# Rewriting most stages of a decoder layer: biases in PSUM, quarter-array scores, norms on GpSimd, one GELU, a 16-bit down product

## Chip, cores and metric

The kernel runs on one core of one Trainium2 chip. The metric is the device time of the whole program in microseconds (us). The engines are PE (TensorE), DVE (VectorE), ACT (ScalarE), POOL (GpSimd) and SP (SyncE, which only issues DMA here).

## What is computed

One pre-norm decoder layer on x of shape (16, 64, 256):

```python
x = x + attn(layernorm(x))        # 16 heads of 16, causal, ALiBi, Wq/Wk/Wv/Wo with biases
x = x + xattn(layernorm(x), ctx)  # softmax(x @ ctx.T / 16, masked) @ ctx, one head of 256
x = x + ffn(layernorm(x))         # gelu(x @ up + b) @ down + b, F = 1024

def quantize_to_mxfp4(w, block_size=32):     # both FFN weights, at run time
    wb = w.reshape(K // 32, 32, N)
    scales = 2 ** (floor(log2(max(abs(wb), axis=1))) - 2)
    q = nearest value of (0, 0.5, 1, 1.5, 2, 3, 4, 6) with sign, of wb / scales
    return q, scales                          # the product uses q * scales
```

## The kernel before

The 1024 tokens lie in 8 tiles of 128 (two batches of 64 each), `x_sb`. The program is a list of named stages. `stages()` gives each its engine, an estimated time, what it must follow and which PSUM banks it writes; `schedule()` lays them out greedily with a time for each, with `URGENCY` as a table of priorities; every engine then walks the one list and issues its own stages in that order. Semaphores do the waiting.

- Layer norm (LN1, LN2, LN3), per tile: `stats` and `norm` on DVE (L776, L777, L785), `rstd` on POOL (L528, L532), `turn` transposes on PE (L932), `turn_copy` on ACT (L573, L576). For LN3, `low` on DVE (L791) keeps the rest that 16 bits lose, since the up product runs twice in fp16, high and low.
- Projections per half (4 tiles), with fp32 weights: `q` and `k` (L945) and `v` (L955). The keys are copied from `k_flat` into `k2`, 8 masked copies of 512 columns for each half and chunk `c`, on ACT (L598) and DVE (L799), shared out by `K_HEADS`: copy j keeps head j's 16 rows of the 128 and zeroes the others. So one product of `q_T` with `k2` gives eight heads' scores. The values go to `v2` half by DVE (L812), half by ACT, a DMA between partitions and ACT again (L609, L623).
- Attention in 16 units (tile, c): `scores` (L969), two products for the two batches, each 128 rows by 64 columns of the array with 512 columns streamed, into bank 0 or 1; `add_max` on DVE adds the ALiBi and causal table and takes the maximum (L825, L828); `centre` on POOL subtracts it (L556); `exp` on ACT (L629); `prob_T`, `prob_copy`, `pv`, `normalise`, `attn_turn`, `attn_copy` (L977, L636, L990, L838 and L839, L999, L643); per tile `out_proj` and `x1` (L1006, L846).
- Cross-attention per tile: `x_scores`, `x_mask` (adds the mask and takes the maximum on DVE, L865 and L869), `x_exp`, `x_prob_T`, `x_read`, `x_scale` (with the product with `valid`, L876), `x2`.
- Quantising: `amax`, `binade` and transposes give scales, `spread` (L1046, L1051) spreads them over rows. `quant` is four blocks on DVE, two per weight matrix, each of eight operations on two pieces of 512 columns and one on 1024 (L734 to L762). `raw` is one buffer, loaded four times.
- FFN in 32 blocks (4 groups of two tiles, 8 chunks): `up` (L1064, 4 products of 256 columns), `gelu` twice on ACT from the same bank (L688: one rounded to fp32r as `h_hi`, one full as `h_sb`), `split` on DVE (L902, the difference, `h_lo`), `down` (L1080, 4 fp32r products), then `final` (L909) and the store.

The stage of the scores, and the table which shares out the keys:

```python
for b in range(2):
    tok = slice(t * P + b * S, t * P + (b + 1) * S)
    last = pe.matmul(dst[b * S:(b + 1) * S, :].rearrange("p (h k) -> p h k", h=HC), q_T[:, c, tok],
                     k2[:, c, :, tok], start=True, stop=True)
...
K_HEADS = {(0, 0): 3, (0, 1): 3, (1, 0): 4, (1, 1): 4}
```

## Time and profile before

| | us |
|---|---|
| median of 3 runs (lowest, highest) | 159.94 (157.6, 162.42) |
| span of the profiled execution, first to last instruction | 157.1 |
| lowest run above that span | 0.5 |
| median run above that span | 2.8 |

The times of the three runs are of whole executions. The profile is of one execution, of which the page gives the span; what lies around it isn't given for it, so the differences above are to other executions. A duration in the profile is that of one instruction; on PE the ends are modelled and neighbours overlap, so the time that a matmul takes in a row of others is better read from one start to the next. An fp32 matmul shows as two records.

### The profile page before, as it was taken

How to read it: one execution, taken by the hardware profiler on the slowest of the kernel's cores; microseconds unless marked ns; L12 is line 12 of the kernel's file. 1: busy time of each engine (PE TensorE's matmuls, PEld its weight loads, DVE VectorE, ACT ScalarE, POOL GpSimd, SP SyncE). 2: the span in 40 equal slices, each digit the busy share in tenths (PEclk: the TensorE clock that was granted, in tenths of full speed). 3: DMA queues.
4: the chain of work that ended last, by engine and by line, in shares of the span. 5: the costliest groups of instructions: out<-in, count | busy, mean ns of one | idle time of the engine just before them, and what ended most of it. 6: DMA issues, size and time to landing. Idle time of an engine off the chain costs nothing. (4 is left out here: it accounts for less than half of the span.)

```text
span 157.1 us, 2931 instructions
## 1 busy us (share of the span) xinstructions
PE 127.9 (81%) x878; PEld 87.3 (56%) x878; DVE 126.1 (80%) x345; ACT 96.4 (61%) x212; POOL 54.1 (34%) x92
## 2 busy tenths in 40 slices
PE   0149999987992497991977999898999999979992
PEld 0027444312471174550565657677788989759991
DVE  1854998799999999779899988796785789697551
ACT  3014559996936045582322742666989899899970
POOL 8969920052211240310403343732540254052000
PEclk9999999999999789998579999999999999999999
DMA  4999993000020341910000000000000000020011
GB/s 95 321 329 341 368 274 144 2 2 4 2 67 0 87 180 30 280 30 0 0 0 4 0 0 0 4 2 0 4 0 2 4 33 31 3 73 0 0 67 67
DMA packets 9135, 11.20 MB, mean 71 GB/s; under 512 B 1665, under 2 KB 7937, under 8 KB 8993
## 3 DMA queue, kind: packets, MB, share of 16 engines
q1 hardware_dynamic: 7776, 9.90, 20.3%
q10 hardware_dynamic: 1344, 1.13, 2.2%
q8 instruction: 7, 0.11, 0.3%
q14 instruction: 8, 0.06, 0.1%
HBM read 9.45 MB, written 1.05 MB: 67 GB/s over the span
## 5 line engine op out<-in xcount | busy, mean ns | idle before, releaser
L556 POOL TENSOR_TENSOR s_sb<-s_sb,s_max 128x512 f32<-128x512 f32 x16 | 17.3, 1084 | 50.1 <-DVE s_max L828 50.1
L969 PE MATMUL bank<-k,q_T 128*64 128x512 f32 x64 | 20.0, 681 | 5.2 <-DVE s_sb L825 5.2
L1064 PE MATMUL bank<-xn_T,w_T 128*128 128x256 f16 x128 | 19.2, 273 | 1.2 <-ACT h_sb L688 0.7
L1080 PE MATMUL bank<-w_down_q,h_hi 128*128 128x256 f32 x64 | 18.7, 318 | 0.0
L636 ACT ACTIVATE p_T<-bank 128x512 f32<-128x512 f32 x16 | 9.6, 599 | 13.1 <-PE bank L990 10.3
L932 PE MATMUL bank<-const,xn 128*128 128x128 f32 x48 | 10.3, 304 | 8.8 <-DVE xn L785 8.7
L990 PEld LDWEIGHTS bank<-v,p_T 128*64 128x64 f32 x256 | 14.1, 148 | 5.9 <-issue 4.7
L902 DVE TENSOR_TENSOR h_lo<-h_sb,h_hi 128x256 fp32r<-128x256 f32 x32 | 13.4, 437 | 4.8 <-ACT h_sb L688 4.8
L528 POOL TENSOR_SCALAR var_eps<-mean_var 128x1 f32<-128x1 f32 x24 | 5.8, 240 | 31.7 <-DVE mean_var L777 31.6
L688 ACT ACTIVATE h_hi<-bank,bias_cols 128x256 fp32r<-128x256 f32 x32 | 15.3, 478 | 2.3 <-PE bank L1080 0.7
L990 PE MATMUL bank<-v,p_T 128*64 128x34 f32 x256 | 15.7, 235 | 1.2 <-ACT q_T L643 1.1
L1080 PE MATMUL bank<-w_down_q,h_lo 128*128 128x256 f32 x64 | 16.3, 282 | 0.0
L945 PE MATMUL bank<-xn_T,w_T 128*128 128x512 f32 x32 | 15.0, 600 | 0.3 <-ACT q_T L582 0.2
L688 ACT ACTIVATE h_sb<-bank,bias_cols 128x256 f32<-128x256 f32 x32 | 15.2, 475 | 0.0
L785 DVE TENSOR_SCALAR xn<-x_sb,mean_var,rstd 128x256 f32<-128x256 f32 x24 | 12.6, 524 | 3.1 <-PE bank L932 2.0
L532 POOL TENSOR_TENSOR rstd<-var_eps,minus_half 128x1 f32<-128x1 f32 x24 | 13.8, 575 | 2.0
L629 ACT ACTIVATE s_sb<-s_sb 128x512 f32<-128x512 f32 x16 | 10.0, 624 | 6.5 <-POOL s_sb L556 6.4
L776 DVE BATCH_NORM_STATS2 stats<-x_sb 128x6 f32<-128x256 f32 x24 | 10.0, 416 | 4.5 <-DMA x_sb<-in_x_dram 4.5
L932 PEld LDWEIGHTS bank<-const,xn 128*128 128x128 f32 x48 | 6.4, 153 | 12.5 <-issue 9.6
L1064 PEld LDWEIGHTS bank<-xn_T,w_T 128*128 128x128 bf16 x128 | 10.9, 97 | 4.4 <-issue 2.6
L1080 PEld LDWEIGHTS bank<-w_down_q,h_hi 128*128 128x128 f32 x64 | 12.1, 190 | 0.3
L1080 PEld LDWEIGHTS bank<-w_down_q,h_lo 128*128 128x128 f32 x64 | 12.2, 190 | 0.1
(82 smaller groups left out, 271.6 us busy)
## 6 DMA issues: line engine op xcount, KB each, us to landing
raw<-in_W_up_T_dram SPq DMA_DIRECT2D x1, 1024.0 KB, 10.5
ctx_T<-in_ctx_by_feature_dram SPq DMA_DIRECT2D x1, 1024.0 KB, 9.7
ctx_sb<-in_ctx_dram SPq DMA_DIRECT2D x1, 1024.0 KB, 9.9
raw<-in_W_up_dram SPq DMA_DIRECT2D x1, 1024.0 KB, 4.9
raw<-in_W_down_T_dram SPq DMA_DIRECT2D x1, 1024.0 KB, 4.8
raw<-in_W_down_dram SPq DMA_DIRECT2D x1, 1024.0 KB, 6.6
out_dram<-x_sb SPq DMA_DIRECT2D x8, 128.0 KB, 1.7
x_sb<-in_x_dram SPq DMA_DIRECT2D x4, 128.0 KB, 3.1
```

What stands on the lines that cost most here:

```text
L532: pool.tensor_tensor(rstd[:, n, t:t + 1], var_eps[:, n, t:t + 1], minus_half[:, :], ALU.pow).then_inc(rstd_ready[n], 1)
L556: pool.tensor_tensor(tile, tile, s_max[:, u % S_RING, :].unsqueeze(2).broadcast_to([P, HC, S]), ALU.subtract).then_inc(centred, 1)
L629: act.activation(s_sb[:, u % S_RING, :], s_sb[:, u % S_RING, :], ACT.Exp).then_inc(exp_ready, 1)
L688: act.activation(dst, bank[i % 2][:, 0:GN], ACT.Gelu_apprx_tanh, bias=bias_cols[:, BUP + f:BUP + f + 1], scale=1.0 / ACT_SCALE).then_inc(g ...
L785: dve.tensor_scalar(xn[:, ring[t % len(ring)], :], x_sb[:, t, :], mean_var[:, n, t, 0:1], rstd[:, n, t:t + 1], ALU.subtract, ALU.mult).the ...
L902: dve.tensor_tensor(h_lo[:, i % H_RING, :], h_sb[:, i % GELU_RING, :], h_hi[:, i % H_RING, :].bitcast(F32), ALU.subtract).then_inc(split_r ...
L932: last = pe.transpose(dst[:, c * P:(c + 1) * P], xn[:, ring[t % len(ring)], c * P:(c + 1) * P], ident)
L945: last = pe.matmul(dst[:, :], w_T[:, m, i, c * P:(c + 1) * P], half_tokens(h, i), start=(i == 0), stop=(i == EC - 1))
L969: last = pe.matmul(dst[b * S:(b + 1) * S, :].rearrange("p (h k) -> p h k", h=HC), q_T[:, c, tok], k2[:, c, :, tok], start=True, stop=True)
L990: last = pe.matmul(dst[b * S:(b + 1) * S, g * width:(g + 1) * width], p_T[:, u % 2, g, b * S:(b + 1) * S], v2[:, 2 * t + b, c * 4 + g, :, ...
L1064: last = pe.matmul(dst[:, 0:GN], w_up_q[:, c, f * P:(f + 1) * P], xn_T16[:, g * GT:(g + 1) * GT, at16:at16 + P], start=(k == 0), stop=(k = ...
L1080: last = pe.matmul(dst, src[:, i % H_RING, t * P:(t + 1) * P], w_down_q[:, f, :], start=(f == 0 and part == 0 and t == 0), stop=(f == FC - ...
```

## The change

Nearly all stages are rewritten, and the order is new:

- The ALiBi and causal table is split once into a high fp32r part and its rest (`bias_hi` on ACT, `bias_lo` on DVE) and added by PE: `s_bias`, a product of `twin` and `s_bias` into the bank, ahead of the scores. `scores` is now per tile for both units: 8 products of 64 rows, 64 columns of the array and 256 streamed columns, over the array's four quarters; `k2` has 4 masked copies (`SLOTS`) in place of 8. DVE takes the maximum from PSUM (`s_max`) and subtracts it (`s_sub`); `centre` is gone.
- The 16 key copies are shared among ACT (5), DVE (4) and POOL (7) by `K_ENGINE`; the key bias goes into `k_flat`.
- `v` writes even heads to partitions 0 to 63 and odd ones to 64 to 127, in products of 64 columns of the array; `v_even` (ACT) and `v_odd` (DVE) copy them in place, with no DMA. The value bias is folded into bo (`bo_fold`, `bo_sum`).
- The norms of LN2 and LN3 are on POOL, with a `shift` before them. `attn_turn` and `attn_copy` are per tile. The mask of the cross-attention is added by PE from a 16-bit product; `valid` is in the scale of `x_prob_copy`.
- Quantising is single stages (`quant`, 10 and 11 steps) of 2048 columns (the first two of 1024) in order with others; W_up has two buffers, `raw_T` and `raw`, and both its loads are issued at the start.
- FFN in 24 blocks: one group of 4 tiles (512 columns), two of 2. One GELU; `hi` (ACT in the first 8 blocks, POOL in the 16 behind them) scales it to fp16, `lo` (DVE) takes the rest, and `down` is 16-bit: fp16 times bf16.

```diff
+GROUPS = ((0, 1, 2, 3), (4, 5), (6, 7))
+K_ENGINE = {(0, 0): ("act", "act", "dve", "dve"), (0, 1): ("act", "pool", "dve", "dve"),
+            (1, 0): ("pool", "pool", "pool", "act"), (1, 1): ("pool", "pool", "pool", "act")}
+HI_ENGINE = ["act" if i < FC else "pool" for i in range(len(BLOCKS))]
...
 URGENCY = {
-    "x_fill": 23, "add_down": 23, "v2_zero": 22, "norm": 18, "q": 17, "turn": 16, "attn_copy": 14,
...
+    "add_bo": -20.1, "add_down": -25.3, "amax": 1.3, "attn_copy": -12.8, "attn_turn": -57.7, "bias_hi": 20.5,
...
+                if stage == "s_bias":
+                    t, r = at
+                    pe.wait_ge(twin_ready, 1)
+                    pe.wait_ge(s_bias_lo, 1)
+                    dst = claim(r, (subtracted, EC * t + r + 1))
+                    pe.matmul(dst[:, :], twin[:, :], s_bias[:, r * HU * S:(r + 1) * HU * S], start=True, stop=False,
+                              skip_group_check=True)
...
-                    dst = claim(u % 2, (scores_added, u + 1))
-                    for b in range(2):
-                        tok = slice(t * P + b * S, t * P + (b + 1) * S)
-                        last = pe.matmul(dst[b * S:(b + 1) * S, :].rearrange("p (h k) -> p h k", h=HC), q_T[:, c, tok],
-                                         k2[:, c, :, tok], start=True, stop=True)
+                    for c in range(EC):
+                        for r in range(EC):
+                            for b in range(2):
+                                tok = slice(t * P + b * S, t * P + (b + 1) * S)
+                                part = slice(r * S, (r + 1) * S)
+                                last = pe.matmul(
+                                    bank[r][b * S:(b + 1) * S, c * SLOTS * S:(c + 1) * SLOTS * S].rearrange(
+                                        "p (h k) -> p h k", h=SLOTS),
+                                    q_T[part, c, tok], k2[part, c, :, tok], start=False, stop=(c == EC - 1),
+                                    skip_group_check=True)
...
+                if stage == "norm" and at[0] != LN1:
...
+                    pool.tensor_scalar(xn[:, ring[t % len(ring)], :], x_sb[:, t, :], rstd[:, n, t:t + 1],
+                                       shift[:, n, t:t + 1], ALU.mult, ALU.add).then_inc(xn_ready[n], 1)
...
+                    for j in k_slots(h, c, "pool"):
+                        last = pool.tensor_scalar(k2[:, c, j, h * HT:(h + 1) * HT], k_flat[:, c, :],
+                                                  slot_mask[:, j:j + 1], 1.0, ALU.mult, ALU.mult)
...
-                    for dst in (h_hi[:, i % H_RING, :], h_sb[:, i % GELU_RING, :]):
-                        act.activation(dst, bank[i % 2][:, 0:GN], ACT.Gelu_apprx_tanh, bias=bias_cols[:, BUP + f:BUP + f + 1],
-                                       scale=1.0 / ACT_SCALE).then_inc(gelu_ready, 1)
+                    act.activation(h_sb[:, i % H_RING, 0:n], bank[i % 2][:, 0:n], ACT.Gelu_apprx_tanh,
+                                   bias=bias_cols[:, BUP + f:BUP + f + 1], scale=1.0 / ACT_SCALE).then_inc(gelu_ready, 1)
...
+                    pool.tensor_scalar(h_hi[:, i % H_RING, 0:n], h_sb[:, i % H_RING, 0:n], h_factor[:, :], 1.0,
+                                       ALU.mult, ALU.mult).then_inc(hi_ready["pool"], 1)
...
+                    dve.scalar_tensor_tensor(out=h_lo[:, i % H_RING, 0:n], in0=h_sb[:, i % H_RING, 0:n],
+                                             scalar=h_factor[:, :], in1=h_hi[:, i % H_RING, 0:n], op0=ALU.mult,
+                                             op1=ALU.subtract).then_inc(lo_ready, 1)
```

Where the order moves. DVE in the middle of attention, before: a whole block of quantising between the maximum of one unit (`s_max`) and the bias of the next.

```order
L828 TENSOR_REDUCE s_max<-s_sb 128x8
L734 TENSOR_SCALAR h_sb<-raw 128x512 x2
L739 TENSOR_SCALAR h_sb<-q_scale 128x512 x2
L742 TENSOR_TENSOR h_sb<-h_sb 128x512 x2
L745 TENSOR_SCALAR h_sb<-h_sb 128x512 x2
L748 TENSOR_SCALAR q_big<-h_sb 128x512 x2
L750 TENSOR_TENSOR h_sb<-h_sb,q_big 128x512 x2
L752 TENSOR_TENSOR h_sb<-h_sb,q_big 128x512 x2
L754 TENSOR_SCALAR h_sb<-h_sb 128x512 x2
L760 TENSOR_TENSOR w_T<-h_sb,q_scale 128x1024
L825 TENSOR_TENSOR s_sb<-bank,alibi_sb 128x512
L828 TENSOR_REDUCE s_max<-s_sb 128x8
```

And now, in the stretch where the quantising of W_up goes on (`q_code`, `q_x`, 2048 columns):

```order
L875 TENSOR_TENSOR s_sb<-bank,s_max 128x512
L867 TENSOR_REDUCE s_max<-bank 128x8
L886 RECIPROCAL s_inv<-bank 128x8
L887 TENSOR_TENSOR attn<-bank,s_inv 128x128
L875 TENSOR_TENSOR s_sb<-bank,s_max 128x512
L785 TENSOR_SCALAR q_code<-q_scale 128x2048
L788 TENSOR_TENSOR q_x<-q_x,q_code 128x2048
L867 TENSOR_REDUCE s_max<-bank 128x8
L886 RECIPROCAL s_inv<-bank 128x8
L887 TENSOR_TENSOR attn<-bank,s_inv 128x128
L875 TENSOR_TENSOR s_sb<-bank,s_max 128x512
L867 TENSOR_REDUCE s_max<-bank 128x8
```

The nine operations no longer stand in one piece; each is a stage between maxima, subtractions and normalising.

PE from the first v product (`w_T,xn_T`) to the first scores (`k,q_T`), before; the names are v, turns (`const,xn`), projections (`xn_T,w_T`) and scale transposes (`const,binade`):

```order
L955 MATMUL bank<-w_T,xn_T 128x256 x4
L932 MATMUL bank<-const,xn 128x128 x6
L945 MATMUL bank<-xn_T,w_T 128x512 x2
L932 MATMUL bank<-const,xn 128x128 x2
L945 MATMUL bank<-xn_T,w_T 128x512 x2
L932 MATMUL bank<-const,xn 128x128 x2
L945 MATMUL bank<-xn_T,w_T 128x512 x2
L932 MATMUL bank<-const,xn 128x128 x2
L945 MATMUL bank<-xn_T,w_T 128x512 x6
L1036 MATMUL bank<-const,binade 8x128 x4
L969 MATMUL bank<-k,q_T 64x512 x2
L945 MATMUL bank<-xn_T,w_T 128x512 x2
```

And now, behind the first v product and two projections, down to the first scores, with the bias products (`s_bias,twin`):

```order
L995 MATMUL bank<-const,xn 128x128 x2
L1017 MATMUL bank<-xn_T,w_T 128x512 x2
L995 MATMUL bank<-const,xn 128x128 x2
L1017 MATMUL bank<-xn_T,w_T 128x512 x2
L995 MATMUL bank<-const,xn 128x128 x2
L1030 MATMUL bank<-w_T,xn_T 64x128 x16
L1017 MATMUL bank<-xn_T,w_T 128x512 x2
L1040 MATMUL bank<-s_bias,twin 128x512
L1130 MATMUL bank<-const,binade 8x128 x4
L1040 MATMUL bank<-s_bias,twin 128x512
L1017 MATMUL bank<-xn_T,w_T 128x512 x2
L1054 MATMUL bank<-k,q_T 64x256 x8
```

One v product more and two bias products stand ahead of the first scores; the number of projections ahead of them is six in both.

POOL behind the norms of LN1, before: four additions of bo and the first eleven `centre`.

```order
L520 TENSOR_TENSOR x_sb<-x_sb,row_biases_all 128x256 x4
L556 TENSOR_TENSOR s_sb<-s_sb,s_max 128x512 x11
L528 TENSOR_SCALAR var_eps<-mean_var 128x1
L532 TENSOR_TENSOR rstd<-var_eps,minus_half 128x1
L528 TENSOR_SCALAR var_eps<-mean_var 128x1
L532 TENSOR_TENSOR rstd<-var_eps,minus_half 128x1
L556 TENSOR_TENSOR s_sb<-s_sb,s_max 128x512 x3
```

And now: key copies, additions, then the chains of LN2, each with its norm.

```order
L611 TENSOR_SCALAR k<-k_flat,const 128x512 x7
L618 TENSOR_TENSOR x_sb<-x_sb,row_biases_all 128x256 x8
L576 TENSOR_SCALAR var_eps<-mean_var 128x1
L580 TENSOR_TENSOR rstd<-var_eps,minus_half 128x1
L584 TENSOR_SCALAR shift<-mean_var,rstd 128x1
L594 TENSOR_SCALAR xn<-x_sb,rstd,shift 128x256
L576 TENSOR_SCALAR var_eps<-mean_var 128x1
L580 TENSOR_TENSOR rstd<-var_eps,minus_half 128x1
```

`centre` is gone from POOL, and a `shift` and a norm of 128x256 end each chain.

## Rows read from the trace of the kernel before

**Rows 1.** The page's first part: busy time, share of the span and instructions of each engine.
```profile
PE 127.9 (81%) x878; PEld 87.3 (56%) x878; DVE 126.1 (80%) x345; ACT 96.4 (61%) x212; POOL 54.1 (34%) x92
```

**Rows 2.** Windows at 28, 104 and 154.1 us: busy PE, PEld, DVE, ACT, POOL; PEclk; DMA.
```profile
0.00:28.00 28.00, 17.90 (x52) 9.53 (x52) 19.39 (x49) 12.38 (x22) 17.96 (x36) 1.00 0.82 263
28.00:104.00 76.00, 61.84 (x425) 36.48 (x424) 69.17 (x179) 41.14 (x86) 22.42 (x29) 0.93 0.13 36
104.00:154.10 50.10, 48.14 (x405) 41.33 (x403) 36.77 (x119) 42.84 (x106) 13.73 (x27) 1.00 0.05 17
```

**Rows 3.** Timeline of DVE, first and last line of a quantising block: start, duration, instruction.
```profile
46.40 1.60 DVE L734 TENSOR_SCALAR h_sb<-raw 128x512 uint16<-128x512 uint16 x2
...
51.72 0.69 DVE L760 TENSOR_TENSOR w_T<-h_sb,q_scale 128x1024 bf16<-128x1024 bf16 x1
```

**Rows 4.** Timeline of PE: v product, projections, scores behind a wait, scores and spread.
```profile
11.11 3.35 PE L955 MATMUL bank<-w_T,xn_T 128*128 128x256 f32 x7 [1.22 <-DMA w_T<-in_W_vo_T_dram]
...
13.40 1.49 PE L955 MATMUL bank<-w_T,xn_T 128*128 128x256 f32 x3
...
18.49 1.88 PE L945 MATMUL bank<-xn_T,w_T 128*128 128x512 f32 x4
20.21 0.38 PE L932 MATMUL bank<-const,xn 128*128 128x128 f32 x2
...
53.15 1.98 PE L969 MATMUL bank<-k,q_T 128*64 128x512 f32 x4 [5.16 <-DVE s_sb L825]
...
65.81 1.08 PE L969 MATMUL bank<-k,q_T 128*64 128x512 f32 x4
66.82 0.39 PE L1051 MATMUL bank<-scale_T,rows 32*128 32x256 bf16 x2
```

**Rows 5.** Groups by line and shape on DVE: busy us, mean ns, idle before and releaser.
```profile
L825 DVE TENSOR_TENSOR s_sb<-bank,alibi_sb 128x512 f32<-128x512 f32 x16 | 10.9, 684 | 0.7 <-PE bank L977 0.5 <-PE bank L969 0.2
...
L799 DVE TENSOR_SCALAR k<-h_sb,const,bk_masked 128x512 f32<-128x512 f32 x18 | 9.3, 581 | 1.6 <-ACT h_sb L591 1.6
...
L734 DVE TENSOR_SCALAR h_sb<-raw 128x512 uint16<-128x512 uint16 x8 | 4.7, 634 | 1.3 <-DMA raw<-in_W_down_dram 1.3
...
L750 DVE TENSOR_TENSOR h_sb<-h_sb,q_big 128x512 bf16<-128x512 bf16 x8 | 3.0, 413 | 0.0
...
L865 DVE SCALAR_TENSOR_TENSOR xs_sb<-bank,x_mask 128x128 f32<-128x128 f32 x8 | 2.3, 285 | 0.3 <-PE bank L1015 0.2
...
L876 DVE TENSOR_TENSOR xs_scale<-xs_inv,valid 128x1 f32<-128x1 f32 x8 | 2.2, 276 | 0.3
...
L754 DVE TENSOR_SCALAR h_sb<-h_sb 128x512 bf16<-128x512 bf16 x8 | 1.9, 281 | 0.0
...
L760 DVE TENSOR_TENSOR w_T<-h_sb,q_scale 128x1024 bf16<-128x1024 bf16 x2 | 1.4, 692 | 0.2
```

**Rows 6.** Durations (min/median/max ns) of the split and of the norm on DVE.
```profile
L902 DVE TENSOR_TENSOR h_lo<-h_sb,h_hi x32: 392/418/845, 113.9 to 152.6; 128x256 fp32r<-128x256 f32 x32
...
L785 DVE TENSOR_SCALAR xn<-x_sb,mean_var,rstd x24: 396/408/1970, 5.3 to 140.8; 128x256 f32<-128x256 f32 x24
```

**Rows 7.** Groups by line and shape on ACT: one of the two GELUs.
```profile
L688 ACT ACTIVATE h_hi<-bank,bias_cols 128x256 fp32r<-128x256 f32 x32 | 15.3, 478 | 2.3 <-PE bank L1080 0.7 <-DVE h_lo L902 0.3
```

**Rows 8.** Groups by line and shape on POOL.
```profile
L556 POOL TENSOR_TENSOR s_sb<-s_sb,s_max 128x512 f32<-128x512 f32 x16 | 17.3, 1084 | 50.1 <-DVE s_max L828 50.1
...
L549 POOL TENSOR_TENSOR x_sb<-x_sb,row_biases_all 128x256 f32<-128x256 f32 x8 | 6.0, 744 | 2.4 <-DVE xn L785 2.4
...
L528 POOL TENSOR_SCALAR var_eps<-mean_var 128x1 f32<-128x1 f32 x24 | 5.8, 240 | 31.7 <-DVE mean_var L777 31.6
```

**Rows 9.** The chain that ended last, two of its pieces in the FFN: start, us.
```profile
146.56 0.45 PE bank L1064 x4
147.01 0.48 PE bank L1080 x4
```

**Rows 10.** Timeline of POOL: the second memset of the values.
```profile
5.24 1.91 POOL L537 MEMSET v<- 128x2176 f32 x1
```

More of the change, by code:

```diff
@@ L188, in stages @@
[L188 to L199 removed]
+            add("spread", (i,), "pe", 0.35, [("scale_copy", (m, parts - 1)), ("load_rows", ())], [7], ("spread_copy", (i,)))
@@ L261, in schedule @@
             if all(r in ended for r in readers):
-                starts[key] = max([free_at.get(engine, START_US)] + [ended[o] + hop for o in after + readers])
+                at = START_US if engine in ("pe", "dve", "act", "pool") else 0.0
+                starts[key] = max([free_at.get(engine, at)] + [ended[o] + hop for o in after + readers])
                 if ACT_TABLE.get(key[0], act_table) != act_table:
@@ L283, in schedule @@
                 us /= clock
-        free_at[engine] = start + us
+        free_at[engine] = start + us - OVERLAP.get(engine, 0.0)
         ended[key] = start + us
```

890 lines of the change are left out of this document (486 added, 404 removed).

## The prediction

> **What bounds the kernel now.** Read in this order: the page's first part [rows 1]: PE (TensorE) and DVE are each busy four fifths of the span of 157.1 us, so neither bounds the whole span. The span cut at three events [rows 2]: 28 us, where the first scores are multiplied; 104 us, where the first FFN product starts; 154.1 us, where the last matmul ends. The reader is to see two kernels in one. From 28 to 104 DVE is busy 69.2 of 76 us and PE 61.8, partly at a lower clock (0.93). From 104 on PE is busy 48.1 of 50.1 us and DVE 36.8. The first 28 us are loads, norms and projections, the last 3.0 the residual and its store.
>
> Why PE isn't full in the middle is in the timeline. DVE quantises half a weight matrix in one piece, from 46.40 to 52.4 us [rows 3]; PE has run out of scores and idles 5.16 us, and the scores behind it take 1.98 us where they take 1.08 elsewhere [rows 4]. That is PE's lower level, 1.2 for 2.4 GHz, after that idle. Over 76 us the clock is 0.07 short, 5.3 us; PE was busy for some 80% of that, so about 4.2 of its busy microseconds are lost to the clock, and 14.2 us are idle.
>
> **The change, engine by engine.**
>
> DVE, from [rows 5, 6]. Removed: 16 of 24 norms (0.41 each at the median, 6.6 us); 14 of 18 key copies (9.3 us for 18, so 7.3); the masking of x-scores (2.3) and the product with `valid` (2.2). The quantising has the same operations on 4 times as many columns. Now it is four blocks like the one of 6.0 us [rows 3], 24. One of 1024 columns takes 692 ns where one of 512 takes 413: 279 ns per 512, so 1.25 us for 2048. The 4 strided ones, 634 ns for 512 now, take about 1.15 for 1024 (4.6), 8 two-tensor ones 10.0, 9 one-tensor ones between 0.28 (a whole instruction of 512) and 0.95 (four at the pitch of 1.9/8); I take 0.65, as their rate is double: 5.9. Together 20.5 against 24: 3.5 less. The split's 13.4 (32 at the median of 418) becomes 8 x 0.69 + 16 x 0.42 = 12.2 (the row of the 512-column addition and the split itself): 1.2. The smaller edits on values and amax, whose rows are left out, I count at 1. The addition of the bias and the subtraction of the maximum exchange places: 10.9 either way. Added: `bias_lo` about 1.1 (1024 columns), `bo_sum` 0.42, six tiny operations of `h_scale` about 1.0. Net 22 us less: 126 becomes 104.
>
> ACT, from [rows 7]: 64 GELUs of 0.48 (30.5) become 8 GELUs and 8 copies of 512 columns at about 0.70 (0.48 and an estimated 0.9 ns for each further column) and 16 GELUs of 0.48, together 18.9; 9 of 14 key copies and the copies of moved values go too. It is busy 96 us now [rows 1] and falls below 84; it stays off the path.
>
> POOL, from [rows 8]: 16 `centre` (17.3 us) go. In come 16 norms of 128x256, 7 key copies of 128x512, 16 `hi` of 128x256, all with one tensor in. The trace has none of these: below them stands a 128x1 at 0.24, above them the two-tensor ones at 0.74 and 1.08. I take 0.5, 0.8 and 0.5, nearer the upper rows, plus 0.3 for each `shift`: 54 + 26.4 - 17.3 = 63 us, half of the new span. An LN chain gets longer by about 0.4 us, behind other tiles' work.
>
> PE, from [rows 4] and, for the FFN, [rows 9]. A unit of scores now is 4 records in 1.01 us (65.81 to 66.82), while a projection's 4 records of the same columns take 1.72 (18.49 to 20.21): the two 64-column halves run side by side. Now 16 units cost 16.2. New is a tile in 16 records of 256 columns and 64 rows. One after the other they'd take 16 x 0.215 = 3.44, in pairs 1.72 and more, four at a time 0.86. I take 1.1: today's pairs come within 20% of their ideal, and the new order runs through the four quarters in turn. 8 x 1.1 = 8.8, 7.4 less. The bias product has 512 columns of fp32r: twice the 0.12 of a down product of 256 is 0.24, the 0.39 of a spread product is the upper end; 0.25, 4.0 for 16. The mask product (8 x 0.08) and the bo product (one output projection's, 0.9) add 1.5. FFN: 4 up records take 0.45 us and 4 down 0.47, 0.117 each for 107 ns of columns, so wider blocks and 16-bit weights bring 0.3 at most.
>
> The Trainium skill, "TensorEngine Tiling (Array Packing)", Key Properties, says that 64x64 tiles work independently, but that a change of tiling mode drains the array. By the first a tile would take 0.86; by the second each of the 8 groups pays twice more. The trace shows halves alone and no quarter, so it can't decide.
>
> **The sum.** First scores. The v product starts when W_vo lands, 11.11, and ends at 14.8 as now. Then four q/k, one v and two more q/k at 1.72, 12.0; four turns between them at 0.22, 0.9; two bias products and a scale transpose, 1.0. 28.7 us, against 28.05 now. DVE no longer holds it up: POOL does the four rstd of the first tiles before its second memset, whose like kept a norm waiting for 1.97 us now [rows 6, 10].
>
> PE behind that: 61.8 + 48.1 = 110.0 busy now, less 4.2 for the clock, 105.8. Less 7.4 (scores), 1.7 (one v product more stands ahead of the scores), 0.3 (FFN); plus 3.5 (14 bias products) and 1.5: 101.4 us.
>
> Idle: the 14.2 + 2.0 of now [rows 2] shrink, since quantising comes as single instructions of up to 1.25 us between scores, where it came as a block of 6.0. What is late next? DVE's `w_down_q`, for which the first down product waits: ahead of it, by the new order, DVE has about 69 of the 83 us that it has left at 28.7 (behind it come 20 splits, 8 final adds and three tiles' norms and sums), PE 77 of its 101 (behind it come 128 down products at 0.117, 14 of the up groups at 0.45 and some 3 us for the last tiles). So PE leads by a tenth, and I leave it 3.5 us of idle. End: 28.7 + 101.4 + 3.5 + 3.0 for the final add and store = 136.6. The lowest of three runs is 0.5 above the profiled span, the median 2.8; I add 0.5: 137.
>
> **The rivals.**
>
> A. *Both engines fill up and hand their waits to each other.* PE at 77 and DVE at 69 in one stretch meet through two score banks: a tile's scores can't start before the two subtractions of the tile before are done. For it: DVE at 91% in the middle now leaves PE 14.2 us idle. Against: with 0.9 of PE's load DVE isn't the bound. If 12 us of idle stay instead of 3.5: 145.
>
> B. *POOL and DVE get in each other's way.* The norm of 1.97 us ended 0.15 us after a memset that began 0.1 before it [rows 6, 10]; the split, 418 ns at the median, took up to 845 [rows 6]. New are 39 POOL instructions of half a microsecond or more for 16 of 1.08. In the last 16 blocks DVE's split (0.42) and POOL's `hi` (0.5 to 0.74) alternate: 0.92 to 1.16 per block if neither overlaps, against PE's 0.92. 16 x 0.24 = 3.8, and the same again over norms and quantising: 137 + 4 to 8 = 141 to 145. Against it: scores, maxima and normalising read PSUM.
> The Trainium skill, "GPSIMD Engine Reference", Key points, says that the two share SBUF interfaces and meet when DVE runs in a two-port mode or has two SBUF inputs; by that rule split, key copies and quantising would all be held, the upper end of B; the norm's row agrees.
>
> C. *The other side: quarters don't run side by side.* If 64-row pieces go one after another, a tile takes 3.44, 8 x 2.34 = 18.7 more; the v products in 64 columns likewise, 4 x 1.7 = 6.8; a bias product at 0.39, 2.2. 137 + 27.7 = 165, slower than 159.9 by 3%. It decides from 3.2 us a tile. Against it: halves do overlap today.
>
> D. *PE's busy time has slack.* Busy time counts the tail of each matmul before an idle gap; counted by starts, the stretch holds about 5 us less than 105.8. Then, with a tile at 0.9, 130.
>
> **How the numbers follow.** Forecast 0.50; A 0.22; B 0.15; C 0.03; D 0.10. The likeliest gives 137. The low end, 129, is D with the lower bounds (bias product 0.24, no idle). The high end, 148, takes in A and B together in part; beyond it lie C and A with B in full, about 1 in 10. A measurement of this kernel tells about 2% from no change. All but C end far below 156.7, and I leave 0.03 for a mixture that stops in between: faster 0.94, same 0.03, slower 0.03.
>
> **What would show it.** Right: first scores near 28.7; a tile's 16 score records within 1.2 us; DVE busy 100 to 107 and PE 118 to 125; no PE wait on DVE above 2 us; clock above 0.97; last 16 blocks at 0.93 us. Wrong: a tile of scores above 1.7 (towards C); DVE instructions with one SBUF tensor at twice their median beside POOL's (B); PE below 85% in the middle with DVE above 90% (A); a first down product that waits for `w_down_q` by more than 3 us.

## The result and the profile after

| | before | after |
|---|---|---|
| median of the runs | 160.97 us (157.6 to 162.42, 4 runs) | 144.98 us (144.24 to 149.28, 4 runs) |
| profiled execution, its span | [rows 2] | 144.24 us, 142.2 us |
| first scores | 28.05 us | 31.13 us |
| PE, DVE, POOL busy | [rows 1] | 118.8, 103.7, 74.6 us |

The ratio is 0.912 with a 95% interval of 0.893 to 0.930. The forecast was 137.0 with a range of 129 to 148: the right side and inside the range, but the time is 8 us above the forecast and lies where rivals A and B had put theirs (145, and 141 to 145). One remark is needed to read all times below: some executions of a kernel show a lower granted clock in a stretch and take up to 5 us more, so a median can move by that, and ratios leave those executions out.

The page's first part, its rows of PE, DVE, POOL and clock in 40 slices, and its chain that ended last:

```profile
PE 118.8 (84%) x1034; PEld 81.1 (57%) x1034; DVE 103.7 (73%) x241; ACT 76.0 (53%) x154; POOL 74.6 (52%) x131
...
PE   0045999999999999999778999798882799999981
...
DVE  0539569959538399899697898988799428577662
...
POOL 8745440201553920518278488764899103897760
PEclk9999999999999999999999999999999789999999
...
PE 58%; POOL 19%; DVE 9%; issue 6%; DMA 5%; SPq 1%; ACT 1%; DVEq 1%; POOLq 0%; ACTq 0%
```

DVE fell from 126.1 [rows 1] to 103.7 us, as forecast (104). POOL rose to 74.6, where 63 was forecast, and it now holds 19% of the chain that sets the end. PE has one dark place, slice 31 (a 2), around 107 to 111 us. The span cut at the events of this kernel (columns as in [rows 2]):

```profile
0.00:31.10 31.10, 20.32 (x110) 12.00 (x110) 18.79 (x41) 12.04 (x22) 13.18 (x29) 1.00 0.85 278
31.10:107.00 75.90, 70.36 (x708) 47.41 (x707) 63.36 (x156) 46.66 (x99) 42.72 (x73) 1.00 0.05 16
107.00:110.90 3.90, 1.06 (x5) 0.36 (x5) 3.87 (x7) 1.26 (x2) 3.52 (x4) 1.00 0.00 0
110.90:139.10 28.20, 27.02 (x213) 21.36 (x213) 16.97 (x38) 16.07 (x32) 15.14 (x26) 0.94 0.09 30
139.10:142.20 3.10, 0.02 (x1) 0.00 (x0) 0.76 (x2) 0.00 (x0) 0.00 (x0) 1.00 0.25 85
```

Behind the first scores PE is busy 98.4 us (the second to fourth row) of 108.0: 9.6 us of idle, where 3.5 were forecast. In the third row PE stands still for 2.8 of 3.9 us, and both DVE (3.87) and POOL (3.52) are full: that is where to look. PE's waits, the first of them at the start (tiles to be normed), the second behind it:

```profile
PE bank L995 <- DVE xn L841: 10.7, 3, 7.0
PE bank L995 <- POOL xn L594: 6.0, 7, 2.7
PE bank L1159 <- ACT h_sb L747: 1.4, 3, 0.6
```

L995 is the turning of a normed tile. All seven waits behind the first scores at that line end with a norm on POOL. The timelines of POOL, then DVE, then PE at the longest of them (start, duration in us, instruction, idle before it):

```profile
104.60 1.86 POOL L623 TENSOR_TENSOR x_sb<-x_sb,row_biases_all 128x256 f32<-128x256 f32 x2
106.55 1.07 POOL L576 TENSOR_SCALAR var_eps<-mean_var 128x1 f32<-128x1 f32 x1
107.71 0.57 POOL L580 TENSOR_TENSOR rstd<-var_eps,minus_half 128x1 f32<-128x1 f32 x1
108.38 0.81 POOL L584 TENSOR_SCALAR shift<-mean_var,rstd 128x1 f32<-128x1 f32 x1
109.29 1.52 POOL L594 TENSOR_SCALAR xn<-x_sb,rstd,shift 128x256 f32<-128x256 f32 x1
```
```profile
104.89 0.18 DVE L833 BATCH_NORM_AGGREGATE mean_var<-stats 128x2 f32<-128x6 f32 x1
...
105.80 1.74 DVE L797 TENSOR_TENSOR q_code<-q_x,q_big 128x2048 bf16<-128x2048 bf16 x1
...
108.46 0.68 DVE L799 TENSOR_SCALAR q_x<-q_code 128x2048 bf16<-128x2048 bf16 x1
...
109.73 0.74 DVE L808 TENSOR_SCALAR q_code<-q_x,w_factor 128x2048 bf16<-128x2048 bf16 x1
110.50 1.38 DVE L809 TENSOR_TENSOR w_down_q<-q_code,q_scale 128x2048 bf16<-128x2048 bf16 x1
```
```profile
110.86 0.44 PE L995 MATMUL bank<-const,xn 128*128 128x128 f32 x2 [2.70 <-POOL xn L594]
111.14 3.26 PE L1159 MATMUL bank<-xn_T,w_T 128*128 128x512 f16 x12
114.19 0.42 PE L1176 MATMUL bank<-w_down_q,h_hi 128*128 128x256 bf16 x1
```

A 128x1 operation that takes 0.23 us alone (median 230 ns, below) took 1.07, `shift` 0.81 for 0.27, the norm 1.52 for 0.55, each beside a wide DVE instruction on SBUF. (The second operation, `rstd`, took its usual 0.57.) LN2's chain for tile 7 took 4.27 us (106.55 to 110.82). It also began late: the mean and variance of that tile were ready at 105.07 (first DVE line), but POOL was then busy with two additions of `b_down` (first POOL line), so 1.5 us went by before the chain started. In this execution the clock fell behind the idle time: the down products from 114.19 take 0.42 us for the 0.27 of the others, which is TensorE's 1.2 GHz level, and the window of 28.2 us has 0.94. The changed kernel run again below had the same wait of 2.70 us and a clock of 1.00 throughout, so the wait alone doesn't bring the low clock. Durations on POOL (min/median/max ns) show how far the stretching goes:

```profile
L576 POOL TENSOR_SCALAR var_eps<-mean_var x24: 221/230/1299, 4.3 to 124.3; 128x1 f32<-128x1 f32 x24
...
L584 POOL TENSOR_SCALAR shift<-mean_var,rstd x16: 264/266/1217, 60.1 to 125.3; 128x1 f32<-128x1 f32 x16
L594 POOL TENSOR_SCALAR xn<-x_sb,rstd,shift x16: 548/549/1516, 60.5 to 125.7; 128x256 f32<-128x256 f32 x16
```

### The profile page after: what moved, and what is told of

Its sections match the earlier page's. It is cut to its first block, busy times and chain, and to the rows that moved or that the text cites. A ratio compares the mean times of both kernels' runs of the same rounds, so it can differ in the third digit from the quotient of the medians.

```text
span 142.2 us, 3094 instructions
## 1 busy us (share of the span) xinstructions
PE 118.8 (84%) x1034; PEld 81.1 (57%) x1034; DVE 103.7 (73%) x241; ACT 76.0 (53%) x154; POOL 74.6 (52%) x131
## 4 chain that ended last, share of the span: by engine, by line
PE 58%; POOL 19%; DVE 9%; issue 6%; DMA 5%; SPq 1%; ACT 1%; DVEq 1%; POOLq 0%; ACTq 0%
PE bank L1017 10%; PE bank L1030 6%; PE bank L1159 6%; PE bank L1176 5%; PE bank L1054 5%; DMA x_sb<-in_x_dram 5%; POOL xn L594 4%; POOL shift L584 4%; PE bank L1079 4%; PE bank L995 4%; PE bank L1065 4%; POOL rstd L580 4%; POOL var_eps L576 4%; PE bank L1040 3%; PE bank L1121 2%
## 5 line engine op out<-in xcount | busy, mean ns | idle before, releaser
L995 PE MATMUL bank<-const,xn 128*128 128x128 f32 x48 | 10.6, 311 | 16.7 <-DVE xn L841 10.7
L1159 PE MATMUL bank<-xn_T,w_T 128*128 128x256 f16 (+1 forms) x96 | 18.8, 323 | 1.6 <-ACT h_sb L747 1.4
L964 DVE SCALAR_TENSOR_TENSOR h_lo<-h_sb,h_factor,h_hi 128x256 f16<-128x256 f32 (+1 forms) x24 | 14.4, 608 | 6.3 <-POOL h_hi L632 3.8
L995 PEld LDWEIGHTS bank<-const,xn 128*128 128x128 f32 x48 | 6.0, 151 | 22.5 <-issue 8.6
L747 ACT ACTIVATE h_sb<-bank,bias_cols 128x256 f32<-128x256 f32 (+1 forms) x24 | 12.8, 543 | 7.8 <-PE bank L1159 4.1
L1176 PE MATMUL bank<-w_down_q,h_hi 128*128 128x256 bf16 x64 | 15.5, 278 | 0.5 <-DVE h_lo L964 0.5
L1176 PE MATMUL bank<-w_down_q,h_lo 128*128 128x256 bf16 x64 | 15.3, 277 | 0.0
L867 DVE TENSOR_REDUCE s_max<-bank 128x8 f32<-128x512 f32 x16 | 10.9, 683 | 3.9 <-PE bank L1054 3.9
L594 POOL TENSOR_SCALAR xn<-x_sb,rstd,shift 128x256 f32<-128x256 f32 x16 | 10.1, 631 | 1.7
L875 DVE TENSOR_TENSOR s_sb<-bank,s_max 128x512 f32<-128x512 f32 x16 | 10.9, 681 | 0.0
L1079 PE MATMUL bank<-v,p_T 128*64 128x34 f32 x256 | 10.6, 227 | 0.2 <-DVE attn L887 0.2
L632 POOL TENSOR_SCALAR h_hi<-h_sb,h_factor 128x256 f16<-128x256 f32 x16 | 9.5, 597 | 2.1 <-ACT h_sb L747 2.1
L1065 PE MATMUL bank<-const,s_sb 128*128 128x128 f32 x64 | 10.0, 279 | 0.0
## 6 DMA issues: line engine op xcount, KB each, us to landing
raw<-in_W_up_dram SPq DMA_DIRECT2D x1, 1024.0 KB, 14.6
```

The source lines that it names most:

```text
L594: pool.tensor_scalar(xn[:, ring[t % len(ring)], :], x_sb[:, t, :], rstd[:, n, t:t + 1], shift[:, n, t:t + 1], ALU.mult, ALU.add).then_inc( ...
L747: act.activation(h_sb[:, i % H_RING, 0:n], bank[i % 2][:, 0:n], ACT.Gelu_apprx_tanh, bias=bias_cols[:, BUP + f:BUP + f + 1], scale=1.0 / A ...
L867: dve.tensor_reduce(s_max[:, u, :], bank[u % EC][:, :].rearrange("p (h k) -> p h k", h=HU), AX_X, ALU.max).then_inc(max_ready, 1)
L964: dve.scalar_tensor_tensor(out=h_lo[:, i % H_RING, 0:n], in0=h_sb[:, i % H_RING, 0:n], scalar=h_factor[:, :], in1=h_hi[:, i % H_RING, 0:n] ...
L995: last = pe.transpose(dst[:, c * P:(c + 1) * P], xn[:, ring[t % len(ring)], c * P:(c + 1) * P], ident)
L1065: last = pe.transpose(dst[:, g * P:(g + 1) * P], s_sb[:, u % S_RING, g * P:(g + 1) * P], ident)
```

## The experiments

Twelve runs: the changed kernel again, and eleven variants. The time named first is the median, with the lowest and highest execution behind it. A ratio is to the kernel before, run beside the variant. The level was run beside the first three variants only; medians of the kernel before were 159.5 us there and 160.4, 159.7 and 159.8 beside the later ones, so where a later variant differs from the level by less than 1 us, the times don't settle it.

**The level.** The changed kernel again, beside the first three variants.

> The changed kernel once more, as the level to which the runs beside it are compared. Expected within 1% of the 144.98 us measured for it, with the first scores at about 31.1 us and an idle stretch of PE of 2 to 3 us shortly after 107 us.

Measured: 143.81 us (143.21 to 149.11), ratio 0.905 (0.898 to 0.912); profiled 143.33 with a clock of 1.00, first scores 30.85. Its PE waits behind the start are those above (xn on POOL 6.0, the longest 2.7). All variants below are compared with it, and with its three executions of 143.2 to 144.3.

**Norms of LN2 and LN3 on DVE.**

```diff
-                    if n != LN1:
-                        pool.tensor_scalar(shift[:, n, t:t + 1], mean_var[:, n, t, 0:1], ...
...
-                if stage == "norm" and at[0] != LN1:
-                    pool.tensor_scalar(xn[...], x_sb[:, t, :], rstd[...], shift[...], ALU.mult, ALU.add)
...
-                if stage == "norm" and at[0] == LN1:
+                if stage == "norm":
```

> The 16 norms of LN2 and LN3 stand on DVE instead of POOL, at the same places of the order, and `shift` goes. Theory T (the LN chain on POOL is stretched beside DVE's long two-tensor instructions and ends last for PE: turns waited 6.0 us for POOL's norms): POOL loses 16 x (0.63 + 0.37) = 16 us, DVE gains 16 x 0.41 = 6.6 us (103.7 becomes about 110), PE's waits for xn fall from 6.0 to below 3 us, and the time falls by 1.5 to 4 us, to 141 to 143.5. Rival R (DVE is what is full; 94% busy from 100 to 110 us, so each norm pushes the quantising on): w_down_q ends 2 us later or more than 111.9, and the time stays or rises, 145 to 148.

Measured: 142.64 us (142.26 to 143.68), ratio 0.900 (0.893 to 0.908). POOL 56.1, DVE 108.4. PE's waits for norms behind the start fall from 6.0 to 1.3 us (10.4 in all, 9.1 of them at the start), but 2.5 us of waits for `low` on DVE come in, and the last step of `w_down_q` moves from 110.21 to 112.64. So theory and rival are both half true. The four executions of 142.3 to 143.7 stand against the level's 143.2 to 144.3, some 0.7 us less and below T's 1.5, and the two ratios overlap. Counted from the first scores, the first down product comes at 82.5 us where the level has 82.4: up to there, what POOL's chain gave back DVE's load took. What the profiled execution gains, 1.3 us of span behind the first scores, lies wholly behind that product, where POOL has two tiles' norms less. Even here a tiny POOL operation is held, at the same stretch (POOL, then DVE):

(Alone this operation takes 0.57 us.)

```profile
107.85 1.40 POOL L580 TENSOR_TENSOR rstd<-var_eps,minus_half 128x1 f32<-128x1 f32 x1
```
```profile
107.60 1.22 DVE L783 TENSOR_TENSOR q_code<-q_x,q_big 128x2048 bf16<-128x2048 bf16 x1
```

**Norms on POOL without `shift`.**

```diff
-                    pool.tensor_scalar(xn[...], x_sb[:, t, :], rstd[:, n, t:t + 1],
-                                       shift[:, n, t:t + 1], ALU.mult, ALU.add)
+                    pool.wait_ge(rstd_ready[n], t + 1)
+                    pool.tensor_scalar(xn[...], x_sb[:, t, :], mean_var[:, n, t, 0:1],
+                                       rstd[:, n, t:t + 1], ALU.subtract, ALU.mult)
```

> The norms of LN2 and LN3 stay on POOL, but subtract the mean and multiply by rstd directly, so that the 16 `shift` instructions (mean 0.37 us each with the hop) go. Theory T (POOL's chain is what PE waits for): each chain is 0.3 to 0.5 us shorter, the stall near 107 us is shorter by as much, the time falls by 0.5 to 1.5 us, to 143.5 to 144.5. Rival R (DVE is what is full): the same within 0.3 us of the changed kernel run beside it.

Measured: 145.79 us in the profiled execution (clock 0.988), 149.35 to 151.19 in the three others. Neither theory had this. The group on POOL says why:

```profile
L589 POOL TENSOR_SCALAR xn<-x_sb,mean_var,rstd 128x256 f32<-128x256 f32 x16 | 23.2, 1450 | 1.7
```

The same shape with multiply and add has a median of 0.55 us and a mean of 0.63; with subtract and multiply it takes 1.24 us where no wide DVE instruction is near (84.89, 88.45 and 90.65 us) and 1.91 beside one. So the chain got longer by 0.3 us instead of shorter, and PE's waits for xn rose from 6.0 to 7.4. That fits T, PE pays for time on this chain, and not R; it rests on one execution.

**The second memset later.**

```diff
                     mine = slice(h * B // 2, (h + 1) * B // 2)
+                    if h:
+                        pool.wait_ge(xn_ready[LN1], HALF)
```

> POOL waits before its second memset of v2 (1.91 us) until the norm of the fourth x tile is done; the norm took 1.90 us beside it where its like takes 0.41. Theory M (POOL's memset holds DVE's norm): the norm takes 0.4 us, the v and q/k products and the first scores come 1.3 to 1.6 us sooner (29.5 to 29.8 for 31.1), and the time falls by 1 to 1.5 us. Rival L (what the start waits for is the landing of the x tiles and of W_vo, and DVE's later work is full anyway): the norm is short but the first scores come less than 0.5 us sooner or the end stays within 0.5 us of the changed kernel.

Measured: profiled 148.07 us, the others 143.77 to 149.34, none below the level's lowest. The norm takes 0.41 us (8.81), but the v product started at 12.32 us, when W_vo landed (2.35 us of waiting for that transfer), and the first scores at 31.61. The memset does hold the norm, as M says, but rival L holds for the time: the start is set by the landing. This also corrects a reading of the first profile: there the turn behind the norm of 1.90 us ended last, and v started at 13.14; in after_again, with the same norm of 1.89 us, W_vo's landing did, and v started 0.8 us sooner.

**The bias product in bf16.**

```diff
-        s_bias = sb("s_bias", [P, EC * HU * S], F32R)
-        twin = sb("twin", [P, P], F32R)
+        s_bias = sb("s_bias", [P, EC * HU * S], BF16)
+        twin = sb("twin", [P, P], BF16)
```

> The constant score bias and the 0/1 matrix `twin` are held as bf16 instead of fp32r, so that the bias is a sum of two bf16 numbers in place of an fp32r and its remainder (the bias is less exact than the changed kernel's, everything else is the same). Theory W (the bias product is slow because fp32r passes its 512 columns twice): start to start it falls from about 0.42 us to 0.21 to 0.25, 16 times, so PE has 2.7 to 3.4 us less; the time falls by 2 to 3 us against after_again, to 141 to 142, unless DVE is full. Rival F (fixed cost of loading 128 rows and changing from 64-row pieces, not the type): the product stays above 0.35 us and the time within 0.7 us of after_again. Rival R (DVE or POOL is what is full between 60 and 112 us): the product is short and the time moves by less than 1 us.

Measured: 144.72 us (142.74 to 146.16), ratio 0.895 (0.885 to 0.905). A product's median goes from 498 to 382 ns and its weight load from 186 to 96; start to start 0.34 to 0.42 becomes 0.22 to 0.30. That is 0.12 us each and 1.9 us together, where W claimed 2.7 to 3.4; rival F, which had it above 0.35, falls. The lowest execution is 0.5 us below the level's lowest and the interval overlaps the level's, so the effect on the time isn't settled beyond "small"; part of it lies where PE waits anyway.

**The pv product in the old order.**

```diff
-                    for g in range(4):
-                        for b in range(2):
+                    for b in range(2):
+                        for g in range(4):
```

> The pv product's 8 small matmuls (34 columns, both halves of the output rows) are issued as before the change, all of the one half first and then the other, instead of in turn. Theory P (alternating the halves lets two run side by side, and this is the gain that the forecast didn't have): its start-to-start pitch goes from 0.59 back to about 0.85 us, PE's busy time rises by 4 to 5 us, and the time rises by 2.5 to 4.5 us against after_again. Rival Q (it lies in PE's spare time, since the path runs through DVE and POOL there): the pitch goes back and the time rises by less than 1 us. Rival N (the gain has another cause than the order): the pitch stays at 0.59.

Measured: 148.43 us (146.93 to 150.46), ratio 0.923 (0.912 to 0.934). The groups of the two kernels, level first:

```profile
L1079 PE MATMUL bank<-v,p_T 128*64 128x34 f32 x256 | 10.6, 227 | 0.2 <-DVE attn L887 0.2
```
```profile
L1079 PE MATMUL bank<-v,p_T 128*64 128x34 f32 x256 | 14.6, 227 | 0.4 <-DVE attn L887 0.4
```

One record takes 227 ns in both, but 256 of them take 10.6 or 14.6 us: in turn they overlap more. Theory P holds: two swapped loops are worth 4 us of PE, and the time follows. The three executions of the level from 143.2 to 144.3 stand against 146.9 to 149.1 here, and those of the next variant, run beside this one, are 144.1 to 145.2; that is 3 to 4 us.

**Scores quarter by quarter.**

```diff
-                    for c in range(EC):
-                        for r in range(EC):
-                            for b in range(2):
+                    for r in range(EC):
+                        for b in range(2):
+                            for c in range(EC):
```

> The 16 score matmuls of a tile are issued quarter by quarter (both of a quarter's matmuls in succession, the same rows and output half) instead of running through the four quarters in turn. Theory S (quarters run side by side because neighbours in the order stand on different quarters; two of one quarter can't): a tile takes 1.6 to 2.2 us instead of 1.09, 8 times, so PE has 4 to 9 us more and the time rises by 3 to 8 us against after_again. Rival O (the array takes whatever is queued, in any order, as long as the quarters differ further on): it stays below 1.3 us and the time within 1 us.

Measured: 144.73 us (144.13 to 149.29), ratio 0.901 (0.894 to 0.908). A tile takes 1.11 us where it took 1.09. Theory S falls, rival O holds for a quarter's two matmuls (four records) in succession. Together with the run before: four short matmuls (eight records) of 34 columns on one half in a row cost 4 us over the kernel, two (four records) of 256 columns on one quarter nothing.

**Quantising in halves.** Each step from the third on is two instructions of 1024 columns.

```diff
-                if s == 3:
-                    return dve.tensor_tensor(q_x[:, :], q_x[:, :], q_code[:, :], ALU.mult)
+                for a in range(PIECES):
+                    n = slice(2 * F // PIECES * a, 2 * F // PIECES * (a + 1))
+                    if s == 3:
+                        last = dve.tensor_tensor(q_x[:, n], q_x[:, n], q_code[:, n], ALU.mult)
...
```

> Every step of the quantising from the third on is issued as two instructions of 1024 columns instead of one of 2048. Theory H (a DVE instruction with two SBUF tensors or at double rate holds POOL for its whole length, and POOL's LN chain ends last for PE): the longest POOL instruction of 128x1 falls from 1.3 to below 0.8 us, the var_eps, rstd and shift groups' means fall by 50 ns or more, DVE's busy time rises by 1 to 1.5 us, and the time falls by 0.3 to 1.5 us or stays. Rival R (DVE is what is full): POOL's instructions may be shorter, but the time rises by 0.5 to 1.5 us. Rival G (POOL gets no slot between two DVE instructions in succession): POOL's means stay within 20 ns.

Measured: 142.96 us (142.62 to 148.1), ratio 0.891 (0.885 to 0.897). `var_eps` has a mean of 341 ns for 385, `shift` 448 for 496, DVE 104.9 us busy for 103.8, and the longest PE wait for xn is 2.24 for 2.70. But the longest 128x1 operation still takes 0.97 us, not below 0.8, and two other means rise: `rstd` from 617 to 640 ns, the norm from 631 to 659. The chain of tile 7 takes 3.67 us for 4.26, and the first down product comes 81.8 us behind the first scores where the level has 82.4. DVE does more work and the kernel is no slower: three executions of 142.6 to 143.0 against the level's 143.2 to 144.3, and a ratio whose interval lies just below the level's. H holds in sign, for `var_eps`, `shift` and the time, and not in its sizes; R falls, and so does G.

**W_down not rounded.**

```diff
+                if m == DOWN and s in (5, 6, 7):
+                    return dve.tensor_scalar(h_bound[:, 0:1], h_bound[:, 1:2], 1.0, None, ALU.mult)
```

> Left out: the rounding of W_down (steps 5, 6 and 7 of its quantising, one single-rate and two two-tensor instructions of 2048 columns, become three tiny ones), so the weights are scaled and clipped but not rounded. DVE has 3.0 to 3.4 us less, all of it between 98 and 110 us. Theory AB (the stall of PE at 107 to 110.6 us comes from DVE's quantising, by its time and by holding POOL's chain for tile 7): the stall falls from 2.7 to below 1 us, w_down_q is done near 108, and the time falls by 2 to 3.5 us against after_again, to 140 to 141.5. Rival C2 (the stall is the latency of tile 7's own chain, projection, LN2, cross attention, LN3, and would be there with an idle DVE): the turn of LN2 comes less than 0.7 us sooner and the time falls by less than 1 us.

Measured: 143.44 us (141.33 to 145.73), ratio 0.887 (0.878 to 0.895). The two executions at full clock take 141.3 and 141.8, some 2 us less than the level; the profiled one is 141.82 with the first scores at 31.66, 0.8 us later than the level. Behind the first scores the span is 108.1 us where the level has 110.4: 2.3 us less, for 3.1 us less of DVE. PE's waits, its turning of tile 7, and two operations of that tile's chain on POOL:

```profile
PE bank L997 <- DVE xn L843: 10.2, 3, 7.6
PE bank L997 <- POOL xn L594: 3.6, 7, 0.8
```
```profile
109.06 0.44 PE L997 MATMUL bank<-const,xn 128*128 128x128 f32 x2 [0.37 <-POOL xn L594]
```
```profile
106.25 0.23 POOL L576 TENSOR_SCALAR var_eps<-mean_var 128x1 f32<-128x1 f32 x1
...
107.59 1.41 POOL L594 TENSOR_SCALAR xn<-x_sb,rstd,shift 128x256 f32<-128x256 f32 x1
```

The wait of 2.70 us is 0.37. The chain takes 2.75 us for 4.26. Theory AB holds for the stall: it came from DVE's quantising, though the instruction that PE waited for stood on POOL. One part of AB failed: `w_down_q` was to be done near 108 and ends at 111.47, where the level has 111.59. DVE had idle time here (1.34 us before 106.98). Of the 2.3 us that PE no longer waits, 1.5 are the shorter chain on POOL; the rest was gained ahead of it. The two additions still stand ahead of the chain (it starts at 106.25 with the mean ready at 104.90), and no run moves them alone. Rival C2 falls.

**Three versions meant to be the best.** All have the bf16 bias, halves, the later memset, and a new start:

```diff
-            act.dma_start(w_T[:, WQ:WK + 1, :, :], ...).then_inc(qk_loaded, 16)
             act.dma_start(w_T[:, WV:WO + 1, :, :], ...).then_inc(vo_loaded, 16)
+            act.dma_start(w_T[:, WQ:WK + 1, :, :], ...).then_inc(qk_loaded, 16)
...
+    for item, before in ((("v", (0, 0)), ("turn", (0, 2))),
+                         (("bias_hi", ()), ("q_copy", (0, 0))),
+                         (("bias_lo", ()), ("norm", (0, 7))),
+                         (("add_down", (0,)), ("hi_pool", (10,))),
...
+        order.remove(item)
+        order.insert(order.index(before), item)
```

(`alibi` is loaded behind the row biases.) The last row stands for seven additions.

> A version meant to beat both: W_vo is loaded before W_qk and the alibi table behind x's second half and the small tables; the first v product stands before the third turn, bias_hi and bias_lo later; the second memset of v2 waits for the fourth norm; the score bias is bf16; quantising is in halves; the b_down additions of tiles 0 to 6 come after the last LN3 norm, where POOL is idle. Norms stay on POOL. By parts: start 1.5 to 2.5 us sooner (first scores at 28.4 to 29.4), bias product 2 us of PE's time, of which part lies in idle time, halves 0.5, the additions out of POOL's chain 0.5 to 1. Together 3 to 5 us: 138.5 to 140.5. Rival K (the clock falls in a stretch of small matmuls as it does in some executions of bias_bf16): 142 or more.

> As combo_pool, with the norms of LN2 and LN3 on DVE and without `shift`. Where POOL's stretched chain is what PE waits for, it beats combo_pool by about the 1 us that norm_dve gained, 137.5 to 139.5; where halves and later additions have already taken that away, DVE's 6.6 us more make it slower than combo_pool by 0.5 to 1.5 us.

Measured: combo_pool 144.09 us (143.42 to 144.33), ratio 0.902 (0.896 to 0.908); combo_dve 144.17 (142.85 to 145.89). By their medians both are 4 to 5 us above what was expected of them and no faster than the changed kernel. The start did what was said: in combo_pool v started at 9.45, the first scores at 29.31 and the first down product at 109.18 for 113.23. Then the lead of 4 us was lost. In combo_pool, a PE wait and what stood on POOL:

```profile
PE bank L1199 <- DVE h_lo L987: 3.5, 2, 3.1
```
```profile
120.00 4.82 POOL L638 TENSOR_TENSOR x_sb<-x_sb,row_biases_all 128x256 f32<-128x256 f32 x7
```

The additions moved in a block ahead of a `hi_pool`, and the mean clock from 120 us to the end was 0.91; up to 120 it was 1.00. In combo_dve the same block left PE waiting 2.4 us for `h_lo`. Rival K had the time right, 142 or more, but not the place: the clock didn't fall among the small matmuls. The third version puts six of them ahead of LN3's tile 6, where POOL was idle for 8.17 us.

```diff
-                         (("add_down", (0,)), ("hi_pool", (10,))),
+                         (("add_down", (0,)), ("rstd", (LN3, 6))),
...
```

> As combo_pool, but the six b_down additions of tiles 0 to 5 stand on POOL before the rstd of LN3's tile 6, where combo_pool's trace had POOL idle for 8.17 us, instead of between the last norm and the third `hi_pool`, where they held the hi copies for 4.82 us and PE for 3.1 us. Theory (that wait and the low clock behind it are the whole reason why combo_pool didn't keep its lead of 4.05 us at the first down product): no PE wait on h_lo above 1 us, first down product at 109.0 to 109.8 us, and behind it the same 28.1 us as in after_again: span 137.2 to 138.2, time 139 to 140.3. Rival (the lead is given back in the last blocks whatever stands there, by POOL's and DVE's load): 142 to 144 again.

Measured: 144.02 us (141.06 to 145.94), profiled 143.64. Neither: the wait on h_lo is gone, and instead PE waited 2.50 us for `w_down_q` (first down product at 112.53), because POOL's block now held DVE. Another 1.4 us went in a wait for `s_sub` at 35 us, before the block, which combo_pool didn't have. POOL, then DVE:

```profile
107.05 6.01 POOL L637 TENSOR_TENSOR x_sb<-x_sb,row_biases_all 128x256 f32<-128x256 f32 x6
```
```profile
107.28 1.21 DVE L986 SCALAR_TENSOR_TENSOR h_lo<-h_sb,h_factor,h_hi 128x512 f16<-128x512 f32 x1
108.41 1.81 DVE L823 TENSOR_SCALAR q_code<-q_x,w_factor 128x1024 bf16<-128x1024 bf16 x2
110.25 2.22 DVE L830 TENSOR_TENSOR w_down_q<-q_code,q_scale 128x1024 bf16<-128x1024 bf16 x2
```

In quant_halves the same three take 0.75, 1.01 and 1.29. They lost 2.2 us, and POOL's six additions took 1.0 each for 0.73. The lowest execution of all, 141.06 at full clock, is of this version, but its median isn't better than the changed kernel's. Among the versions that compute the whole layer, two are a little faster in most of their executions: norm_dve (142.3 to 143.7 in four) and quant_halves (142.6 to 143.0 in three of four); by less than 1 us, and the two weren't run beside each other.

## Why the prediction was right in side and range, and 8 us off

By its own steps, with the profiled execution (142.2 span, 144.24):

| term | forecast | measured | difference |
|---|---|---|---|
| first scores | 28.7 | 31.1 | +2.4 |
| PE busy behind | 101.4 | 98.4 | -3.0 |
| idle behind | 3.5 | 9.6 | +6.1 |
| final add and store | 3.0 | 3.1 | +0.1 |
| outside the span | 0.5 | 2.0 | +1.5 |
| sum | 137.1 | 144.2 | +7.1 |

*The step that failed is the idle term*, "So PE leads by a tenth, and I leave it 3.5 us of idle". It weighed the total load of two engines ahead of one event and took the POOL chain as hidden ("An LN chain gets longer by about 0.4 us, behind other tiles' work"). Of the 9.6 us of idle, 6.0 are PE's seven waits for norms on POOL; the other 3.6 are about as much as was forecast. The longest wait, 2.7 us, is for tile 7, the last, and no other tile's work ran beside it. quant_skip (2.3 us) shows that DVE's quantising makes this wait, and quant_halves and noshift move it the way that goes with it; norm_dve shows that without POOL's chain `w_down_q` on DVE ends last instead. A part of the stall is the order of the list, on two engines. On POOL the tile's chain stood for 1.5 us behind two additions. On PE the up products of two FFN blocks (1.5 us, from 110.85 us on in the level) stand right behind the turn that waits, and need only two banks whose GELUs had ended at 107.3 and 109.1. What moving either alone would give wasn't tried.

*That the time lies inside the range is in part luck.* The forecast left out a gain of 4 us in the pv product (below), which hid part of the idle time. The kernel without that gain, pv_outer, takes 146.9 to 149.1 us, at the high end of the range.

*POOL 63, measured 74.6.* The single prices were right: norm 0.55 for 0.5, `hi` 0.48 alone for 0.5, `shift` 0.27 for 0.3, a key copy 0.77 for 0.8. The miss is the stretching: (384 - 230) ns x 24 + (496 - 266) x 16 + (631 - 549) x 16 + (597 - 480) x 16 + (836 - 730) x 8 = 11.4 us, with means and undisturbed values of this kernel. That is nearly the whole difference of 11.6.

*Rival B was right in its mechanism and wrong in its victim and place.* It was priced as DVE's splits in the last 16 blocks, 0.92 to 1.16 us per block, "and the same again over norms and quantising"; the blocks run at 0.87. DVE's sum came out at 103.7 as forecast, though not part by part: the splits took 14.5 us for 12.2, the quantising 19.7 for 20.5. The one that pays most is POOL, in operations too short to be noticed, and it hurts where PE waits for an LN chain. The Trainium skill, "GPSIMD Engine Reference", Key points, weighed ahead, names exactly the two kinds of DVE instruction; the trace agrees, with 1.30 us for a 128x1 `var_eps` that began with a two-tensor instruction of 1.22 (both at 64.45). The Trainium skill, "SBUF — State Buffer", section "SBUF: two separate sides", calls it a lock for the length of a whole instruction; the runs agree in both directions (in combo_2 three steps on DVE took 5.24 us for 3.05 beside POOL's additions, in memset_later a norm fell from 1.89 to 0.41 once the memset was moved away).

*Rival A was the other half.* It was given 145 for "waits handed to each other", and that is what norm_dve showed: POOL's waits gone, 2.5 us of DVE's in their place. Its own place, the two score banks, isn't where it happened in the changed kernel: no PE wait for `s_sub` is among those of the profile (combo_2 has one, of 1.4 us).

*First scores.* The v product started at 13.14 (forecast 11.11, when W_vo landed before the change). Two things came together there, within some 0.2 us. W_vo took 10.9 us from issue to landing instead of 8.9; the likely reason is that 512 KB of `alibi` had moved ahead of x's second half, an edit on SP's queue that the forecast left out, but W_up's second load and larger tables are new at the start too, and none was tried alone. And the sentence "DVE no longer holds it up" was wrong: the fourth tile's norm stood beside the second memset after all (DVE, then POOL):

```profile
10.57 1.90 DVE L841 TENSOR_SCALAR xn<-x_sb,mean_var,rstd 128x256 f32<-128x256 f32 x1 [0.53 <-PE bank L995]
```
```profile
10.41 1.91 POOL L599 MEMSET v<- 128x2176 f32 x1
```

The runs put the weight on the landing: in memset_later the norm is short, v starts when W_vo lands (12.32), and the first scores are no sooner. The combos, which changed the order of loads and products together, had their first scores at 28.8 to 29.4.

*PE busy.* A tile of scores was forecast at 1.1 and takes 1.09 (1.03 start to start), against 3.44 in series: C falls. The Trainium skill, "TensorEngine Tiling (Array Packing)", Key Properties, had the quarters independent (0.86 by that alone) and the change of mode costly; the trace agrees with the first and leaves at most 0.17 per tile for the second. Missed: the alternating halves of pv, 4 us of gain, two swapped loops in the new kernel that the forecast priced at nothing; the bias product, 0.25 taken, 0.34 to 0.42 measured, about the upper end of the stated bounds, 1.8 us in 14; FFN blocks at 0.87 for 0.93 gave 1 to 2 us back, the lower clock took 1.5 (27.02 busy for the 25.49 of the execution at full clock in the same window).

*Outside the span.* I added the smallest of the three runs' differences to one span, 0.5; the profiled execution's own is 2.0 us. The kernel before, beside the variants, has 1.9 to 2.5.

Open: how much of the 4 us gained at the first down product can be kept. The combos lost it mainly through one block of additions, at two places; leaving these where the changed kernel has them, with all else as in combo_2, wasn't tried.

## What to carry to other kernels

- Moving work to GpSimd to relieve VectorE isn't free when VectorE runs wide SBUF instructions: price each small GpSimd operation on a path with the longest VectorE instruction that may stand beside it (here 1.2 us on 0.23), and count that chain for the last tile, which nothing hides.
- When idle time is forecast from loads, look at the last event of each kind, not at the sum: near 107 us two chains ended within about 1 us of each other (110.8 and 111.9), so each fix alone gave from under 1 to 2 us, and moved blocks came back as another wait.
- Short matmuls on different column halves (here 34 columns) want to alternate in program order; two loops swapped gave 4 us of PE. For matmuls of 256 columns on quarters the order made no difference.
